# Batch norm statistics of seven batches taken during batch 0's attention, table rows sent through product buffers, next batch's first chunk placed beside the offsets

## What is computed

```python
x = x + local_attention(_gn(x), w_qkv, w_kg, b_kg, alpha, beta, w_proj)   # layer 0
x = x + _modulated_dcn(_gn(x), w_off, b_off, w)                           # layer 1

def _gn(v, G=32, eps=1e-5):          # statistics over 8 channels x 64 x 64 pixels of one batch
    g = v.reshape(B_, G, C_ // G, H_, W_)
    return ((g - mean(g)) / sqrt(var(g) + eps)).reshape(v.shape)
```

## Time and profile before

| what | us |
|---|---|
| median of 3 runs (5559.25 to 5576.94) | 5566.27 |
| the profiled execution, own time | 5572.84 |
| its span, first to last instruction | 5571.0 |
| TensorE busy in the span | 5047.5 |
| VectorE busy | 4417.5 |
| ScalarE busy | 2259.6 |

### The profile page before, as it was taken

How to read it: one execution, slowest core, us unless ns; L and a number is a source line. 1 busy time by engine, 2 the same in 40 slices (tenths; PEclk the granted TensorE clock), 3 DMA queues, 4 the chain that set the end, 5 groups by cost and what they waited for, 6 DMA issues and landing times. The chain is left out here.

```text
span 5571.0 us, 89316 instructions
## 1 busy us (share of the span) xinstructions
PE 5047.5 (91%) x31448; PEld 2784.7 (50%) x31448; DVE 4417.5 (79%) x11412; ACT 2259.6 (41%) x4716; POOL 2262.0 (41%) x2311
## 2 busy tenths in 40 slices
PE   7969998999989999899998999989998899988888
PEld 4535554455544555445554455544554455544343
DVE  4546888878887788877888788887878878888998
ACT  2234433444344343444434444334444344444454
POOL 0003334434344333443444444434434344344776
PEclk9979999999999999999999999999999999999999
DMA  2046778967788676886779877787778877678999
GB/s 98 24 134 231 246 236 303 335 221 247 239 320 309 217 256 231 319 296 229 250 239 331 279 235 256 261 309 267 253 240 285 303 251 257 233 274 317 374 397 354
DMA packets 493543, 1456.44 MB, mean 261 GB/s; under 512 B 45732, under 2 KB 115628, under 8 KB 492844
## 3 DMA queue, kind: packets, MB, share of 16 engines
q0 software_dynamic: 331776, 1208.11, 62.5%
q1 hardware_dynamic: 161324, 242.62, 12.3%
HBM read 1313.96 MB, written 136.59 MB: 260 GB/s over the span
## 5 line engine op out<-in xcount | busy, mean ns | idle before, releaser
L663 POOL DMA_INDIRECT G<-table,IDX x2304 | 2261.1, 981 | 3276.2 <-DVE V L1301 2501.4
L682 PE MATMUL ps<-VT,s_wconv 128*128 128x512 f32 x4608 | 2262.7, 615 | 51.5 <-DVE R L1101 50.0
L1301 DVE SCALAR_TENSOR_TENSOR V<-G,WT,V 128x256 f32<-128x256 f32 x4608 | 2019.3, 479 | 124.0 <-DVE V L1301 5.0
L1040 ACT ACTIVATE VT<-ps 128x512 f32<-128x512 f32 x1152 | 685.7, 596 | 2472.8 <-PE ps L888 2470.9
L682 PEld LDWEIGHTS ps<-VT,s_wconv 128*128 128x128 f32 x4608 | 824.8, 194 | 862.4 <-issue 809.3
L1294 DVE SCALAR_TENSOR_TENSOR V<-G,WT 128x256 f32<-128x256 f32 x2304 | 1007.3, 478 | 210.3 <-ACT G L1029 157.4
L888 PEld LDWEIGHTS ps<-s_ident,V 128*128 128x128 f32 x4608 | 567.4, 143 | 834.8 <-issue 764.1
L1073 DVE TENSOR_TENSOR E<-ps,s_band 128x512 f32<-128x512 f32 (+1 forms) x1024 | 641.1, 671 | 377.3 <-PE ps L737 200.9
L1029 ACT ACTIVATE G<-G,WT 128x256 f32<-128x256 f32 x1884 | 859.4, 499 | 146.2 <-DMA G<-table,IDX 145.0
L888 PE MATMUL ps<-s_ident,V 128*128 128x128 f32 x4608 | 706.7, 276 | 167.3 <-DVE V L1301 103.1
L715 PE MATMUL ps<-XN,s_wqk 128*128 128x512 f32 x1024 | 491.1, 609 | 40.1 <-ACT XN L933 40.1
(11 more groups left out here) (103 smaller groups left out, 2920.7 us busy)
## 6 DMA issues: line engine op xcount, KB each, us to landing
table<-ACX SPq DMA_DIRECT2D x128, 528.0 KB
G<-table,IDX POOLq DMA_INDIRECT x2304, 6.2
X<-in_x SPq DMA_DIRECT2D x64, 512.0 KB, 9.2
E<-in_x SPq DMA_DIRECT2D x128, 256.0 KB, 9.1
x<-X SPq DMA_DIRECT2D x64, 512.0 KB, 6.4
R<-x SPq DMA_DIRECT2D x64, 512.0 KB, 9.0
out<-R SPq DMA_DIRECT2D x64, 512.0 KB
s_wconv<-in_wconv SPq DMA_DIRECT2D x1, 2304.0 KB, 10.6
```

Of the source, the lines that this page charges most:

```text
L663: e.indirect_dma_start(G[a % NG][:, :], None, T[b % 2], bass.IndirectOffsetOnAxis(ap=IDX[b % 2][:, col:col + 1], axis=0)).then_inc(d_g[a % ...
L682: mm = e.matmul(CV[oh][:, :], s_wconv[:, h, t, oh * P:(oh + 1) * P], VT[U % 2][:, h, :], start=(t == 0 and h == 0), stop=(t == 8 and h == 1))
L1040: e.activation(VT[U % 2][:, :, 2 * P * pair:2 * P * (pair + 1)], BK[banks.place[use]][:, :].rearrange("p (h n) -> p h n", h=2), ACT.Copy). ...
L1301: e.scalar_tensor_tensor(vt[:, :], gt[:, q * C:(q + 1) * C], wt[:, col, q:q + 1], vt[:, :], ALU.mult, ALU.add).then_inc(lerp[q - 1], 1)
```

## The change

- `norm(0, ...)` is run twice instead of eight times: once for batch 0 and once for batches 1 to 7 together, in tiles with 14 columns (`mv1`, `gnt1`, `gn1`). The statistics of batch c + 1 (`stats1(c + 1)`, 8 steps with two `bn_stats` each) are alternated with chunk c of batch 0's attention; their data is loaded, 512 KB at a time, into the six gather buffers `G[4]` to `G[9]`, which no gather uses yet. `norm(0, 1)` stands between the last `mix` and the last `project` of batch 0. No statistics load remains in any later front.
- Batch 0's statistics are taken from the `X` chunks themselves, which are now all loaded as the first thing; the constants are split into nine that the start needs (`d_first`) and eight that come after.
- The three transposed banks of the table go into three buffers of the rotation of eight product buffers `E`; ScalarE waits only for what used the buffer last. Each is written to HBM by two DMAs of its own: six DMAs of a third of the rows per chunk in place of two.
- `qkv(b + 1, 0)` is alternated with chunk 6 of batch b's offset phase, and the first scores with `qkv(b + 1, 1)` with the weights of its last chunk. The first three `X` chunks of the next batch are loaded beside offsets 1 to 3, not after the front.
- The weights that pace the front count neither the start nor the statistics.

The diff, cut to its core ("..." where lines are left out):

```diff
     def norm(j, b):
-        for kind in ("n.aggr", "n.mean", "n.dev", "n.var", "n.root", "n.fin"):
+        if j == 1:
+            yield ("n.aggr", j, b)
+            yield from hop(HOP)
+        for kind in ("n.mean", "n.dev", "n.var", "n.root", "n.fin"):
             yield (kind, j, b)
             yield from hop(HOP)
     def stats1(b):
-        for n in range(4):
-            yield ("st1.load", b, n)
         for c in range(NCH):
             yield ("st1", b, c)
-        yield from norm(0, b)
-        yield IDLE
+            if b > 0 and NCH * b + c + NST < NCH * NB:
+                yield ("st1.load", *divmod(NCH * b + c + NST, NCH))
+        yield ("st1.aggr", b)
...
-    def layer0(b):
-        if b == 0:
-            yield ("fold",)
-            for c in range(3):
-                yield ("load_x", b, c)
-            yield from stats1(b)
-            yield ("load_late",)
-        yield from qkv(b, 0)
+    def first_scores(b):
         for _ in range(FIRST):
             yield IDLE
         yield from alternate(scores(b, 0), qkv(b, 1))
+    def begin():
         for c in range(NCH):
-            if c + 3 < NCH:
+            yield ("load_x", 0, c)
+        yield from stats1(0)
+        yield ("fold",)
+        yield ("setup",)
+        yield from norm(0, 0)
+        yield ("load_late",)
+        for n in range(NST):
+            yield ("st1.load", 1, n)
+        yield from qkv(0, 0)
+        yield from first_scores(0)
...
+    def layer0(b):
+        for c in range(NCH):
+            if b > 0 and c + 3 < NCH:
                 yield ("load_x", b, c + 3)
             now = [mix(b, c)]
             if c + 2 < NCH:
...
+            if b == 0 and c + 1 < NB:
+                now.append(stats1(c + 1))
             yield from alternate(*now)
-        for _ in range(LAST):
-            yield IDLE
+        if b == 0:
+            yield from alternate(hop(LAST), norm(0, 1))
+        else:
+            yield from hop(LAST)
         yield from project(b, NCH - 1)
         yield from norm(1, b)
         yield IDLE
...
+        if b + 1 < NB and 1 <= c <= 3:
+            yield ("load_x", b + 1, c - 1)
...
     def offset_phase(b):
         before = iter(())
         yield ("pd", b, 0)
         yield from hop(HOP)
         for c in range(NCH):
-            yield from alternate(offsets(b, c), before)
+            beside = [qkv(b + 1, 0)] if c == NCH - 2 and b + 1 < NB else []
+            yield from alternate(offsets(b, c), before, *beside)
             before = weights(b, c)
-        yield from before
+        yield from alternate(before, first_scores(b + 1) if b + 1 < NB else iter(()))
     def front(b):
         offsets_run[0] = False
         yield from layer0(b)
         offsets_run[0] = True
-        yield from alternate(offset_phase(b), stats1(b + 1) if b + 1 < NB else iter(()))
...
         offsets_run[0] = False
-        if b + 1 < NB:
-            for c in range(3):
-                yield ("load_x", b + 1, c)
-    steps = list(front(0))
+    steps = list(begin())
+    n = len(steps)
+    steps += list(front(0))
     weigh = lambda s: max(WEIGHT.get(s[0], 0), LEAST)
-    total = sum(weigh(s) for s in steps)
+    total = sum(weigh(s) for s in steps[n:] if s[0][:3] != "st1")
...
                     banks.give(("tp", g, i))
+                    prods.take(("tt", g, i))
...
+            for i in range(3):
+                prods.give(("tt", g, i))
...
-        ACX = sb("ACX", [P, 6 * C])
+        ACX = sb("ACX", [P, 5 * C])
...
-        TT = ACX[0:88, :].rearrange("p (a c) -> p a c", c=C)
...
-                e.wait_ge(st1_done, before[1] + 1)
+                need_rows(e, prods.place[use], before[1])
...
+        def need_rows(e, k, g):
+            n = sum(v == k and key[0] == "tt" and key[1] <= g for key, v in prods.place.items())
+            if n > 0:
+                e.wait_ge(d_t[k], 32 * n)
+        def norm_parts(j, b):
+            if j == 1:
+                return 2 + b, mv, gnt, gn2[b % 2]
+            part = slice(0, 2) if b == 0 else slice(2, 2 * NB)
+            return b, mv1[:, part, :], gnt1[:, :, part], gn1[:, :, part]
...
+        def stat_place(b, c):
+            n = NCH * (b - 1) + c
+            return n % NST, n // NST
...
+            for c in range(NCH):
+                e.dma_start(X[c][:, :, :], chunk_of(x[0, :, :], c)).then_inc(d_x[c], 16)
...
                              (WN[0], wn.rearrange("(m p) i -> p m i", p=P)[:, 0:4, :]),
                              (WN[1], wn.rearrange("(m p) i -> p m i", p=P)[:, 4:6, :]),
                              (WK, wkx.rearrange("(m p) k -> p m k", p=P)),
+                             (s_wv[:, :, 0:C], wv.rearrange("(h p) o -> p h o", p=P))):
+                e.dma_start(dst, src).then_inc(d_first, 16)
+            e.dma_start(row[0:1, 0:36], bkg).then_inc(d_first, 16)
+            e.dma_start(row[0:1, 36:63], boff).then_inc(d_first, 16)
+            e.dma_start(row[0:1, 63:64], alpha).then_inc(d_first, 16)
...
+            for dst, src in ((s_wqk[:, :, :], wqk.rearrange("(h p) o -> p h o", p=P)),
+                             (s_ident[:, :], ident), (s_selx[:, :, :], selx), (s_band[:, :, :], band.bitcast(BF16)),
+                             (s_selp[:, :, :], selp.bitcast(BF16)),
                              (s_wproj[:, :, :], wproj.rearrange("(h p) o -> p h o", p=P)),
-                             (s_ident[:, :], ident), (s_g8[:, :], g8), (s_selx[:, :, :], selx),
-                             (s_selp[:, :, :], selp.bitcast(BF16)), (s_band[:, :, :], band.bitcast(BF16)),
                              (s_selo[:, :], selo), (s_base[:, :, :], base)):
                 e.dma_start(dst, src).then_inc(d_const, 16)
...
-                        e.wait_ge(fill, (b - 1) * NCH + min(c + 2, NCH))
-                        e.wait_ge(d_s[c], 16 * b)
+                    k, n = stat_place(b, c)
+                    if n > 0:
+                        e.wait_ge(st1_done, 2 * (NCH * b + c - NST + 1))
+                    e.dma_start(G[ST + k][:, :].rearrange("p (h n) -> p h n", h=2), chunk_of(x[b, :, :], c)).then_inc(d_st[k], 16)
+                elif kind == "load_x" and s[1] > 0:
+                    b, c = s[1:]
+                    e.wait_ge(fill, (b - 1) * NCH + min(c + 2, NCH))
+                    e.wait_ge(d_s[c], 16 * b)
                     e.dma_start(X[c][:, :, :], chunk_of(x[b, :, :], c)).then_inc(d_x[c], 16)
...
                     g = b * NCH + c
-                    e.wait_ge(*freed(("tp", g, 2)))
                     if b > 1:
                         e.wait_ge(lerp[2], 2 * PAIRS * (b - 1))
-                    for half in range(2):
-                        pos = (RO * c + 1 - half) * EW
-                        dst = T[b % 2][pos:pos + RO * EW, half * C:(half + 1) * C].rearrange("(a p) c -> p a c", p=88)
-                        e.dma_start(dst, TT[:, :, :]).then_inc(d_t[half], 16)
+                    for i in range(3):
+                        e.wait_ge(*freed(("tp", g, i)))
+                        k = prods.place["tt", g, i]
+                        for half in range(2):
+                            pos = (RO * c + 1 - half) * EW + 176 * i
+                            dst = T[b % 2][pos:pos + 176, half * C:(half + 1) * C].rearrange("(a p) c -> p a c", p=88)
+                            e.dma_start(dst, E[k][0:88, :].rearrange("p (a c) -> p a c", c=C)).then_inc(d_t[k], 16)
...
-                            for half in range(2):
-                                e.wait_ge(d_t[half], 16 * NCH * (b + 1))
+                            e.wait_ge(st1_done, 16 * NB)
+                            for k in range(NE_BUF):
...
+                    if kind == "n.mean":
+                        e.wait_ge(aggr[j], 2 * (b + 1) if j == 1 or b == 0 else 2 * NB)
+                    else:
+                        e.wait_ge(nrm, NRM * k + 3)
+                    src = stat[:, :, 0] if kind == "n.mean" else tmp[:, 2, :]
+                    e.matmul(BK[banks.place[use]][:, 0:dst.shape[2]], s_g8[:, :], src, start=True, stop=True).then_inc(filled(use)[0], 1)
...
+                    if n == 0 and g == 0:
+                        e.wait_ge(d_const, 16 * NCONST)
...
                     if c == 0:
-                        e.wait_ge(nrm, NRM * (2 * b + 1))
+                        e.wait_ge(nrm, NRM * (1 if b == 0 else 2))
...
-                    if c > 0:
+                    if g > 0:
                         e.wait_ge(*filled(("sel", g - 1, 1, 3)))
-                    elif b > 0:
-                        for half in range(2):
-                            e.wait_ge(d_t[half], 16 * g)
                     e.activation(CT[:, :], BK[banks.place[use]][:, :].bitcast(BF16)[:, 0:CH], ACT.Copy).then_inc(freed(use)[0], 1)
                 elif kind == "pv":
...
                         e.wait_ge(*filled(use))
-                        if i == 0 and g > 0:
-                            for half in range(2):
-                                e.wait_ge(d_t[half], 16 * g)
```

(26 more changed lines are left out.)

120 lines of the change are left out of this document (49 added, 71 removed).

## The result

The changed kernel takes 5434.44 us (median of 4 runs, 5431.8 to 5436.28), the kernel before on the same chip 5569.12 (4 runs): ratio 0.9759, interval 0.9742 to 0.9776. That is 135 us less, where 161 were forecast. The profiled execution took 5433.98 us over a span of 5432.2, 138.8 less than before's.

What follows compares the result with a forecast made beforehand. TensorE's work was taken to bound convolutions with a front. Front of batch 0 +20, convolution 0 -26, the next five -22 each, batch 6 -45, last 0: -161 us, span 5410, median 5405, range 5345 to 5465 (to 5485 with A and B).

Steps and rivals of the forecast that it cites:

- (a): Start of batch 0's front: first `qkv` earlier, with fewer loads ahead of the norm; -5 us, bounds -8 and +1.
- (b): Batch 0's attention: 56 steps of two `bn_stats`, mostly covered by VectorE's idle time; +15 us, between 0 and +76.
- (c): End of batch 0's attention: `norm(0, 1)` ahead of the last project, a chain of eight small steps; +2.5 us.
- Rival B: Batch 0's attention: each statistics step costs its full time, +76 us for +15; 5466 us, chance 0.09.
- rival D: Batch 0's attention: statistics steps open gaps and TensorE falls to the lower clock, up to +190 us; 5595, chance 0.05.
- (d): Batch 0's offsets: ScalarE's table waits go, winning TensorE's idle time; -10 us, bounds 0 and -16.
- (e): Batch 0's offsets: `qkv(1, 0)` placed ahead of the last offsets; +12 us.
- (f): Before batch 0's first pair: first scores and `qkv(1, 1)` fill the gap, VectorE's first pair behind the last scores; +5 us.
- The jam in pairs 102 to 126: Convolutions' offset phase: statistics loads and table writes stall TensorE; idle -8.5 us in pairs 102 to 108, -6 behind.
- rival A: Convolutions' offset phase: the jam stays elsewhere, gathers hold up pairs, a convolution gains only 10 us; 5479, chance 0.18.
- Pace: Convolutions: the front ends at pair 139, not 134, so five pairs fewer run alone; -2 us each.
- E: Table writes: the smaller DMAs are slower by their issue time and all of it counts, +95 us; 5500, chance 0.03.

Runs made afterwards that it cites:

- kernel with few statistics: The change without Q, with the `bn_stats` of chunks 1 to 7 of batches 1 to 7 replaced by a memset: 5522.93 us, ratio 0.9664.
- S: Part of the change: statistics, start, earlier loads of `X` chunks and the weights pacing the front; put alone on the kernel before: 5446.4 us, ratio 0.9776.
- T: Part of the change: table rows through the product buffers `E`; put alone on the kernel before: 5554.35 us, ratio 0.9964.
- Q: Part of the change: next batch's first chunk and first scores beside the offsets; the changed kernel without it: 5401.67 us, ratio 0.969.
- 2704: Pace weight of the changed kernel, in place of 2976 in the kernel before; S alone with it: 5446.4 us, ratio 0.9776.
- 2976: S alone with the pace weight of the kernel before, 2976 in place of 2704: 5649.06 us, ratio 0.9894 on another chip.
- 2614: The change without Q, with pace weight 2614 in place of 2704, so a front ends with its convolution: 5616.7 us, ratio 0.9821.

## Why the prediction was right, and where it wasn't

Most of it held: the stages in which the time goes, the sign and the sum, within 26 us of 161. But several terms were mis-sized, and some of these errors cancel.

**Start, (a): right.** First `qkv` at 28.8 for 35.5, -6.7 where -5 was said.

**Statistics steps, (b), and norm(0, 1), (c): right in sum.** 298.4 for 281.3 us is +17.1, against 15 + 2.5. The kernel with few statistics prices 49 steps at 16.2 and leaves 3.0 for the other seven and the norm. Rival B wanted +76 and falls. In the part that (b) was read from it is less: 236.2 us for 229.5 with the same 212 us of TensorE's work, and 23.9 us of idle where 30 were forecast. The other 10.4 us come at the end of the attention, and 5.5 of these are TensorE's own time (39.1 busy for 33.6): its granted clock is 0.76 in the last 62.2 us, for 0.79 in the last 51.8 before. So rival D falls as a loss of 190 us, but a few us of its kind are there. The clock, whose two levels are 1.2 and 2.4 GHz, stayed at the upper one for nearly all of the first 236 us (0.99), where TensorE was busy 90%, and went down and up at the end of the attention (0.80 in 265 to 300 us, 0.83 in 300 to 316, 0.62 in 316 to 345, then 1.00), as it did before the change (0.57 and 0.92). There the trace agrees with the oscillation that the page "TensorE: Matmul & The Clock Gate" of the Trainium skill (section HAM oscillation) tells of; 11 us more of idle did not spread it over the stretch.

**Offsets, first chunk and first scores, (d), (e) and (f): right in sum, not in the parts.** -10, +12 and +5 were said, +7 together. With S in place, T and Q move the first pair from 430.8 to 435.6, +4.8. How this divides depends on the order: T first takes 22.5 (to 408.3) and Q then adds 27.3; Q first adds 19.7 (to 450.5) and T then takes 14.9. In both orders (f) was mis-sized: the stretch from the first gather to the first pair is 6.9 us in both kernels without Q, 20.6 with Q and without T, and 23.2 in the changed kernel, 14 to 16 us more where 5 were said. The waits of 410 to 440 us in the changed kernel, here of the gathers and of VectorE,

```profile
POOL G L694 <- DVE V L1339: 13.4, 1, 13.4
DVE E L1089 <- PE ps L773: 10.5, 1, 10.5
```

show the first pair's scaling queued behind the last scores, which the prediction named and priced too low. (e) and (d) were meant for the stage from the first `om` matmul to the first gather. That stage takes 79.2 us with S alone, 56.5 with T, 84.0 with Q and 69.5 with both; so T is worth 14.5 to 22.7 us there, not 10, and Q 4.8 to 13.0, not 12. For T the 23.6 us of waits in the earlier trace rows were as good a guide as TensorE's idle time in one window of the earlier trace rows. With T alone it goes from 76.1 to 63.3 only. In that kernel VectorE has batch 1's `bn_stats` in this stage and waits 7.4 us for their loads; that this is the reason is not shown.

**The jam in pairs 102 to 126: right, and rival A falls.** The forecast wanted its 21.6 us of idle down to 7; 4.9 remain. Convolutions 0 to 5 had one main cause, the burst of loads, where the prediction read the earlier trace rows as two: taking the loads alone away brings 10 a convolution, T alone nothing. What is left of the jam without the loads, 7.4 us in pairs 108 to 126, no run takes apart. Without the burst the table wait is a cause of its own, in batch 0's offsets and in convolution 6.

**Pace: mis-sized.** I took -2; it is worth 0.0118 of the whole time, some 66 us or 9 a convolution, when the statistics are gone (S alone at 2704 and at 2976), 8 by the comparison on one chip, and nothing while they are there. Some of this was to be had from the weights: without its statistics a front of 2644 at the old pace ends at pair 126, not 139, and 13 pairs more run alone, at 0.53 us of idle each by the earlier trace rows some 7 us.

**The attention: idle time taken to stay, or to fall, rose.** This is the largest miss within a middle convolution. 19 us of idle at the end of the attention were to stay and 3 at the start to go, which leaves 20 us ahead of the first table row of convolution 2; there are 27.8. S brings 2 of the 5 us more than before, Q another 2.4. Behind the first table row the forecast's terms (-8.5, -6, -2, +2) leave 13.6 of 28.1 us, and 9.2 are there: the two errors partly cancel. In whole convolutions S alone saves 22.9 us in each of 1 to 5, which is what I gave to S, T and Q together; T adds 1.4, Q takes 5.6 away, and 18.8 remain.

**First scores hidden in the offset phase, -3 there and +2 here: too much.** At the same pace idle in pairs 0 to 12 is 7.6 without Q and 6.6 with it, and behind the first table row 8.2 and 9.2: Q moves 1 us. The rise from 4.9 to 7.6 came with S.

**Convolution 6: mis-sized.** Of -45, -33 were moved work. S and T bring 16.4 (652.3 for 668.7, the stalls: 13 was said); Q brings 21.5. That once the front is used up the pairs are set by VectorE and the gathers, as in the last convolution (VectorE busy 375.9 of 412.7 us), so that TensorE's work taken out is not all time taken out, is argued from that row. The prediction counted one pair and 1 us for this.

**Small writes: no cost found; E falls.** ScalarE waits for none of the six writes of 176 KB a chunk (idle 0.0 at L1031), where the earlier trace rows had 23.6 us in one phase. By the Trainium skill's fixed cost of a DMA ("DMA: Bandwidth & Descriptors", section Anatomy of one DMA, which measured DMAs issued from GpSimd, while these are issued from SP) the prediction estimated some 450 us, had it been engine time; the measured total excludes that, and is in line with the section's own reading of it as mostly time to completion. Splitting the writes with the same buffers was not run by itself, so a few us of gain or loss inside T's -44 stay possible.

**What stays open.** S gives -127, T -19, and both -171, 25 more than their sum; about 12 of these lie ahead of the first pair, by the paragraph on (d). Which step falls badly beside which pair I haven't isolated. The rows say where: at 2976 behind the first table row, at 2614 ahead of it, and with Q ahead of it; the waits name the engines (VectorE's products and `CB` at the end of a head). In the kernel with only `qkv` moved the loss lies in pairs 0 to 12. That Q harms by shifting the attention against the pairs is argued from these rows, not shown.

## What to carry to other kernels

Move loads, not only compute, off a hand-ordered queue: 14 loads in one place held up everything behind them, and where they stood the wait that looked like a buffer's was in the main theirs. When work leaves a stage that is paced by weights, re-time the pace, and compare the stage by its steps: windows cut by pairs hold other steps at another pace, and a wait that has only moved looks like one that is gone. Moving work of the bounding engine from one stage to the next was here less than a zero sum; take that part of a change out by itself before keeping it.

## What the runs showed of the chip beside this

The same last convolution, which no kernel here changes, takes 412 to 413 us on the chip of the first group, 447 to 450 on that of the second and 437 to 440 on the third. Windows of it: the changed kernel's stands above (DMA share 0.97, 376 GB/s); then the kernel before at the slower pace, second group, to within 2 us of its end:

```profile
5266.50:5711.00 444.50, 355.80 (x1152) 172.25 (x1152) 376.41 (x881) 199.68 (x426) 280.41 (x278) 0.93 0.93 347
```

VectorE's busy time is the same to 0.5 us and the number of gathers too; what they move in a microsecond differs, 376 or 347 GB/s, and with it the granted clock, 0.95 or 0.93. The last convolution alone is 33 of the 146 us between the two chips' times of the kernel before. The Trainium skill's page "HBM Reference" (section Specifications) says that two NeuronCores of one domain share their HBM bandwidth; no run here shows whether another core was at work.
